# A conditional matrix product and a LoRA layer: the first condition matrices are loaded straight to their places, the others split a pair at a time by GpSimd

## The chip, the cores and the metric

The kernel runs on one NeuronCore of a Trainium2 chip. The core's engines are named as the profile names them: PE (TensorE, matrix products; PEld are its weight loads), DVE (VectorE), ACT (ScalarE), POOL (GpSimd) and SP (SyncE, which here only issues DMAs). The names with a q behind (ACTq, POOLq) are an engine's sequencer: DMA issues, register loads. The metric is the device time of one execution in microseconds (us).

## What is computed

```
W = weights[condition]                       # 16 matrices 64x64; one of them per batch item, 64 items
y = einsum('bct,bcd->bdt', x, W)             # x is (64, 64, 1024)
logits = y @ gate_w.T                        # 8 experts; the best two, softmax over the two
result = y @ base_w.T + base_b               # 1024 x 1024
result += 2 * sum_e w_full[e] * (y @ lora_A[e].T) @ lora_B[e].T
out = x + result
```

## The kernel before, in words

Two batch items of 64 channels make a pair of 128 rows; there are 32 pairs, n = 4j + c. For each pair PE makes three kinds of product. The **mix** multiplies x by the condition matrices into the PSUM tensor `mixed`. The **projection** (`project`, L594) multiplies y by the 1160 columns of `proj_w` (1024 of the base layer, 128 of LoRA, 8 gates), in 8 blocks k of 128 rows and 3 banks b. The **experts** (L626) add the LoRA part. To keep the precision of float32 with faster fp32r products, each operand is split into a high and a low part (`w_hi`, `w_lo`, `y_hi`, `y_lo`), and three products are made: 72 matrix products of 384 or 392 columns for each pair.

Pairs 0 and 1 are mixed in another way than the rest (`mix_first`, L600): plain float32, x as the weights, a block-diagonal matrix `w_pair` of the two condition matrices as the moving side. Pairs from 2 on (`mix`, L614) have x split into `x_parts` by ACT (`x_high`, L323) and DVE (`x_low`, L424), and `w_sel`, the high and low part of one condition matrix side by side. y then comes out turned, with the low part's share in other partitions: ACT copies that to `y_rest` (`rest`, L328), DVE adds it (`add_rest`, L432), ACT moves 16 pieces (`move`, L336), DVE turns them (`turn`, L440), ACT rounds (`y_high`, L355), DVE subtracts (`y_low`, L447).

All engines run code written out by hand, ordered by semaphores; an engine's instructions run in the order of the code. `step(j, c)` of each engine handles projection n, while the mix of pair n + 1 and the output of pair n - 1 go on beside it. In step n PE first makes the first half of mix n + 1 (for n = 1 only after block k = 0), then waits until DVE's `finish` (L508 for banks 0 and 1, L511 for bank 2) has taken pair n - 2 out of the accumulators, of which there are two sets, and projects.

At the start, SP issues the loads in this order: the conditions `cond_sb`, x of pair 0, block 0 of `w_raw`, x of pair 1, blocks 1 to 7, x of pairs 2 and 3, `lb_raw`, `bias`. ACT issues the load of all condition matrices, `cw` (128 x 1024, 512 KB: the 16 matrices side by side, twice one above the other). PE runs 12 products of zeros (L719) meanwhile. When `cw` has landed, GpSimd and DVE copy the matrices of pairs 0 and 1 into `w_pair` (L278, L520; 64 x 64 each), ACT rounds all of `cw` into `cw_parts` (L359) and DVE subtracts (L524). From then on GpSimd's `select` (L259) copies two 128 x 128 pieces, high and low together, for each pair.

Of the kernel before, what the change touches and what calls it, by code (L numbers as in the profile page):

```python
# [13 lines left out]
P = 128  # L14
# [4 lines left out]
def adaln_ffn_kernel(  # L19
# [47 lines left out]
    with ExitStack() as ctx:  # L67
# [14 lines left out]
        cw = sb("cw", [P, cond_w.shape[1]], F32)  # L82
        cw_parts = sb("cw_parts", [P, 2, cond_w.shape[1]], F32R)
        cond_sb = sb("cond_sb", [1, B], I32)
# [6 lines left out]
        x_parts = sb("x_parts", [P, 2, 2, T], F32R)  # L91
        w_pair = sb("w_pair", [P, 2, P], F32)
        w_sel = sb("w_sel", [P, 2, 2, P], F32R)

# [43 lines left out]
        w_first = sem("w_first")  # L138
        first_lower = sem("first_lower")
        first_upper = sem("first_upper")  # L140
        cw_hi_ready = sem("cw_hi_ready")
        cw_ready = sem("cw_ready")
        ident_zero = sem("ident_zero")
# [5 lines left out]
        x_split = sem("x_split")  # L149
        sel_ready = sem("sel_ready")  # L150
        rest_ready = sem("rest_ready")
        sum_done = sem("sum_done")

        moved = sem("moved")
# [22 lines left out]
        lora_done = sem("lora_done")  # L177
        bias_added = sem("bias_added")
        res_ready = sem("res_ready")

# [13 lines left out]
        WARM = 12  # L194
        CW_HALVES = (slice(0, CONDITIONS * CH // 2), slice(CONDITIONS * CH // 2, CONDITIONS * CH))

        @block.sync
        def _(sp):
            sp.dma_start(cond_sb[:, :], condition).then_inc(cond_in, 16)

            def load_x(j, c):
# [3 lines left out]
            for k in range(KT):  # L205
                sp.dma_start(w_raw[:, k, :], w_blocks[k]).then_inc(w_in[k], 16)
                if k == 0:
                    load_x(0, 1)
            load_x(0, 2)
            load_x(0, 3)  # L210
            sp.dma_start(lb_raw[:, :], lora_b).then_inc(lb_in, 16)
# [30 lines left out]
        def _(pool):  # L242
# [10 lines left out]
            def select(j, c):  # L253

                pool.wait_ge(mix_done, 8 * j + 2 * (c - 2) + 2)
                for b in range(2):
                    cond = pool.value_load(cond_sb[0:1, bass.ds(8 * j + 2 * c + b, 1)], min_val=0,
                                           max_val=CONDITIONS - 1)
                    nc.gpsimd.tensor_copy(w_sel[:, c % 2, b, :].rearrange("p (h d) -> p h d", d=CH),  # L259
                                          cw_parts[:, :, bass.ds(cond * CH, CH)]).then_inc(sel_ready, 1)  # L260

            def add_bias(j, c):
                if c >= 4:
# [6 lines left out]


            pool.wait_ge(cond_in, 16)
            lower = [pool.value_load(cond_sb[0:1, 2 * c:2 * c + 1], min_val=0, max_val=CONDITIONS - 1)
                     for c in range(2)]
            pool.wait_ge(cw_in, 16)
            pool.wait_ge(w_zero, 1)
            for c in range(2):
                nc.gpsimd.tensor_copy(w_pair[0:CH, c, 0:CH], cw[0:CH, bass.ds(lower[c] * CH, CH)]) \  # L278
                    .then_inc(first_lower, 1)
            pool.wait_ge(first_lower, 2)  # L280
            pool.wait_ge(cw_ready, 2)
            select(0, 2)
# [19 lines left out]
        def _(act):  # L302
            act.dma_start(cw[:, :], cond_w).then_inc(cw_in, 16)

# [51 lines left out]

            act.wait_ge(cw_in, 16)
            for cols in CW_HALVES:
                nc.scalar.copy(cw_parts[:, 0, cols], cw[:, cols]).then_inc(cw_hi_ready, 1)  # L359
            y_high_first(0, 0)  # L360
            w_high(0)
            y_high_first(0, 1)
# [8 lines left out]
            x_high(0, 2, first=True)  # L371
            x_high(0, 3, first=True)

            act.wait_ge(w_ready, 2)

            def step(j, c, ahead=True, split=True):
                if ahead:
                    rest(j, c + 1, 0)
                if c == 1:
                    act.wait_ge(lb_in, 16)  # L380
                    nc.scalar.copy(lb_hi[:, :], lb_raw[:, :]).then_inc(lb_hi_ready, 1)
                gate_exp(j, c - 1)
                if ahead:
                    if c >= 2:
                        act.wait_ge(turned, 8 * j + 2 * (c - 2) + 2)
                    move(j, c + 1, 0, range(3))
                    rest(j, c + 1, 1)
                    move(j, c + 1, 0, range(3, 8))
                lowT_high(j, c - 1)
                if ahead:  # L390
                    move(j, c + 1, 1, range(8)).then_inc(moved, 1)
                    y_high(j, c + 1, 0)
                    y_high(j, c + 1, 1)
                if split:
                    x_high(j, c + 3)
# [12 lines left out]
        def _(dve):  # L408
# [89 lines left out]
            def finish(j, c):  # L498
                n = 4 * j + c + 1
                dve.wait_ge(lora_done, n)  # L500
                dve.wait_ge(bias_added, n)
                add_bank(c, slice(0, 2))
                add_bank(c, 2).then_inc(res_ready, 1)

            def add_bank(c, b):
                if type(b) is slice:
# [4 lines left out]
                return nc.vector.tensor_tensor(part, acc[:, c % 2, b, 0:hi - lo], part, ALU.add)  # L511


            dve.wait_ge(cond_in, 16)
            upper = [dve.value_load(cond_sb[0:1, 2 * c + 1:2 * c + 2], min_val=0, max_val=CONDITIONS - 1)
                     for c in range(2)]
            dve.wait_ge(cw_in, 16)
            dve.wait_ge(w_zero, 1)
            for c in range(2):
                nc.vector.tensor_copy(w_pair[CH:P, c, CH:P], cw[CH:P, bass.ds(upper[c] * CH, CH)]) \  # L520
                    .then_inc(first_upper, 1)
            for i, cols in enumerate(CW_HALVES):
                dve.wait_ge(cw_hi_ready, i + 1)
                nc.vector.tensor_tensor(cw_parts[:, 1, cols], cw[:, cols], cw_parts[:, 0, cols].bitcast(F32),  # L524
                                        ALU.subtract).then_inc(cw_ready, 1)

# [61 lines left out]
        def _(pe):  # L588
# [15 lines left out]
            def mix(j, c, b):  # L604
                n2 = 8 * j + 2 * (c - 2)
                pe.wait_ge(x_split, n2 + b + 1)
                pe.wait_ge(sel_ready, n2 + b + 1)
                if b == 1 or c >= 3:
# [21 lines left out]
            def first_step():  # L630
# [7 lines left out]
                for k in range(KT):  # L638
# [11 lines left out]
                    if k == 0:  # L650
                        pe.wait_ge(x_in[1], 16)
                        pe.wait_ge(first_lower, 2)
                        pe.wait_ge(first_upper, 2)
                        mix_first(1, 0)

                        pe.wait_ge(y_ready, 2)
                        mix_first(1, 1)
                        with_w_lo(0)
# [4 lines left out]
            def step(j, c, ahead=True):  # L663
# [3 lines left out]
                if c >= 2:  # L667

                    pe.wait_ge(res_ready, s - 1)
                for k in range(KT):  # L670
                    if k % HALF_K == 0:
                        pe.wait_ge(y_ready, 2 * s + k // HALF_K + 1)
                    for product in range(3):
                        for b in range(3):
                            done = project(c, k, b, product)

# [43 lines left out]
            pe.wait_ge(x_in[0], 16)  # L720
            pe.wait_ge(first_lower, 1)
            pe.wait_ge(first_upper, 1)
            mix_first(0, 0)
# [41 lines left out]
```

## Time and profile before

| | us |
|---|---|
| median of 3 runs | 498.06 |
| lowest, highest | 498.01, 498.44 |
| the profiled execution: time | 497.86 |
| its span (first to last instruction) | 495.7 |
| PE busy in the span | 491.1 (99%) |
| ACT, DVE, POOL busy | 380.5, 362.6, 123.7 |

PE's clock was granted in full over the whole span. Times below are from the start of the span. Of the profiled execution's 497.86 us, 2.2 lie outside the span. PE is busy nearly all the time, so the few stretches in which it waits, and the time at which its first product starts, are what the other engines can change.

### The profile page before, as it was taken

To read this page: it belongs to the slowest core of one execution; us is meant where nothing else is said; L and a number is where in the kernel's file an instruction comes from. 1 tells how busy PE (TensorE), PEld (TensorE's weight loads), DVE (VectorE), ACT (ScalarE), POOL (GpSimd) and SP (SyncE) were. 2 spreads that over 40 slices of the span, in tenths; PEclk is the share of its full clock that TensorE was granted. 3 is DMA by queue.
4 is the path that set the end of the run, shared out by engine and by line. 5 is a ranking of instruction groups with operands and counts; after the bars stand their busy time and mean duration, and the time that the engine had idled before them with its cause. 6 is when DMAs were issued, how large, how long until landed. Compare 5 with 4: busy or idle time off the path is not lost.

```text
span 495.7 us, 8620 instructions
## 1 busy us (share of the span) xinstructions
PE 491.1 (99%) x2800; PEld 482.8 (97%) x2800; DVE 362.6 (73%) x771; ACT 380.5 (77%) x740; POOL 123.7 (25%) x111
## 2 busy tenths in 40 slices
PE   8999999999999999999999999999999999999997
PEld 8999999999999999999999999999999999999997
DVE  4977878778777778787777777787877777877653
ACT  4888777878778887778787788787788877887620
POOL 2033311333203333113332123331133330233130
PEclk9999999999999999999999999999999999999999
DMA  8812112122122121121221221211211211211112
GB/s 334 347 42 88 56 72 86 43 87 86 42 85 84 43 85 59 68 85 46 81 85 42 85 85 42 85 70 57 85 59 68 85 49 78 85 42 44 45 42 85
DMA packets 11105, 40.07 MB, mean 81 GB/s; under 512 B 1234, under 2 KB 1618, under 8 KB 11090
## 3 DMA queue, kind: packets, MB, share of 16 engines
q1 hardware_dynamic: 10946, 39.36, 21.3%
q10 hardware_dynamic: 144, 0.52, 0.3%
q8 instruction: 8, 0.13, 0.1%
q14 instruction: 7, 0.06, 0.0%
HBM read 23.10 MB, written 16.78 MB: 80 GB/s over the span
## 4 chain that ended last, share of the span: by engine, by line
PE 97%; ACT 2%; DVE 1%; issue 0%; POOL 0%; ACTq 0%; POOLq 0%
PE acc L594 80%; PE acc L626 9%; PE mixed L614 6%; ACT y_moved L336 1%; PE acc L719 1%; PE acc L620 1%; PE mixed L600 1%; ACT w_raw L328 0%; DVE w_raw L508 0%; DVE w_raw L511 0%; DVE y_turned L440 0%; ACT y_hi L355 0%; ACT y_hi L313 0%; ACT w_hi L309 0%; ACT lowT_hi L348 0%
## 5 line engine op out<-in xcount | busy, mean ns | idle before, releaser
L336 ACT COPY y_moved<-w_raw 32x256 f32<-32x256 f32 x480 | 194.2, 405 | 38.4 <-DVE w_raw L432 32.3
L594 PE MATMUL acc<-w_hi,y_hi 128*128 128x384 f32 (+1 forms) x768 | 182.2, 342 | 0.6 <-ACT w_hi L309 0.3
L594 PE MATMUL acc<-w_hi,y_lo 128*128 128x384 f32 (+1 forms) x768 | 179.1, 338 | 0.0
L594 PE MATMUL acc<-w_lo,y_hi 128*128 128x384 f32 (+1 forms) x768 | 179.0, 338 | 0.0
L268 POOL TENSOR_TENSOR w_raw<-x_sb,bias 128x1024 f32<-128x1024 f32 x32 | 77.3, 2417 | 353.8 <-DVE low L488 267.1
L594 PEld LDWEIGHTS acc<-w_hi,y_hi 128*128 128x128 f32 x768 | 135.4, 188 | 8.3 <-issue 0.8
L594 PEld LDWEIGHTS acc<-w_hi,y_lo 128*128 128x128 f32 x768 | 138.5, 188 | 0.1
L594 PEld LDWEIGHTS acc<-w_lo,y_hi 128*128 128x128 f32 x768 | 138.5, 188 | 0.0
L432 DVE TENSOR_TENSOR w_raw<-mixed,w_raw 64x1024 f32<-64x1024 f32 x60 | 73.0, 1217 | 40.7 <-ACT w_raw L328 40.3
L440 DVE STREAM_TRANSPOSE y_turned<-y_moved 128x512 f32<-128x512 f32 x60 | 39.2, 691 | 53.9 <-ACT y_moved L336 53.9
L424 DVE TENSOR_TENSOR x_parts<-x_sb,x_parts 64x1024 fp32r<-64x1024 f32 x60 | 74.0, 1233 | 1.9
L328 ACT COPY w_raw<-mixed 64x1024 f32<-64x1024 f32 x60 | 60.8, 1013 | 17.7 <-PE mixed L614 16.4
L323 ACT CAST x_parts<-x_sb 64x1024 fp32r<-64x1024 f32 x60 | 62.8, 1047 | 1.2 <-DMA x_sb<-in_x 0.3
L355 ACT CAST y_hi<-y_turned 128x512 fp32r<-128x512 f32 x60 | 36.4, 622 | 25.0 <-DVE y_turned L440 25.0
L259 POOL CAST w_sel<-cw_parts 128x128 fp32r x60 | 46.0, 794 | 3.9 <-PE mixed L600 3.6
L447 DVE TENSOR_TENSOR y_lo<-y_turned,y_hi 128x512 fp32r<-128x512 f32 x60 | 41.2, 686 | 4.5 <-ACT y_hi L355 0.5
L614 PE MATMUL mixed<-x_parts,w_sel 128*128 128x512 f32 x120 | 37.6, 395 | 0.0
L508 DVE TENSOR_TENSOR w_raw<-acc,w_raw 128x768 f32<-128x768 f32 x31 | 29.5, 950 | 1.9 <-PE acc L626 1.9
L626 PE MATMUL acc<-lb_hi,lowT_lo 128*128 128x384 f32 (+1 forms) x96 | 30.6, 319 | 0.0
L626 PE MATMUL acc<-lb_lo,lowT_hi 128*128 128x384 f32 (+1 forms) x96 | 30.5, 318 | 0.0
L626 PE MATMUL acc<-lb_hi,lowT_hi 128*128 128x384 f32 (+1 forms) x96 | 30.4, 317 | 0.0
L614 PEld LDWEIGHTS mixed<-x_parts,w_sel 128*128 128x128 f32 x120 | 21.9, 187 | 0.1
(49 smaller groups left out, 241.5 us busy)
## 6 DMA issues: line engine op xcount, KB each, us to landing
x_sb<-in_x SPq DMA_DIRECT2D x32, 512.0 KB, 3.3
out<-w_raw SPq DMA_DIRECT2D x31, 512.0 KB, 2.6
w_raw<-in_proj_w SPq DMA_DIRECT2D x8, 580.0 KB, 9.6
cw<-in_cond_w ACTq DMA_DIRECT2D x1, 512.0 KB, 3.6
lb_raw<-in_lora_b SPq DMA_DIRECT2D x1, 512.0 KB, 16.3
bias<-in_base_b SPq DMA_DIRECT2D x1, 512.0 KB, 17.0
out<-w_raw SPq DMA_DIRECT2D x2, 192.0 KB, 1.9
out<-w_raw SPq DMA_DIRECT2D x1, 128.0 KB, 2.0
```

The source lines that it names most:

```text
L259: nc.gpsimd.tensor_copy(w_sel[:, c % 2, b, :].rearrange("p (h d) -> p h d", d=CH), cw_parts[:, :, bass.ds(cond * CH, CH)]).then_inc(sel_re ...
L268: nc.gpsimd.tensor_tensor(res[:, c % 4, :], x_sb[:, c % 4, :], bias[:, :], ALU.add) \
L323: nc.scalar.copy(x_parts[half, c % 2, b, :], x_sb[half, c % 4, :]).then_inc(x_hi_ready, 1)
L328: nc.scalar.copy(y_rest[:, b, :], mixed[CH:P, :, :]).then_inc(rest_ready, 1)
L336: done = nc.scalar.copy(y_moved[q * SQ:(q + 1) * SQ, g, :, :], piece.rearrange("m (k q a) -> m q k a", q=QUARTERS, a=SQ)[:, q, :, :])
L424: nc.vector.tensor_tensor(x_parts[there, c % 2, b, :], x_sb[here, c % 4, :], x_parts[here, c % 2, b, :].bitcast(F32), ALU.subtract).then_i ...
L432: nc.vector.tensor_tensor(y_sum[:, b, :].rearrange("m (h t) -> m h t", h=2), mixed[0:CH, :, :], y_rest[:, b, :].rearrange("m (h t) -> m h ...
L440: nc.vector.transpose(y_turned[:, :, ks, :], y_moved[:, :, ks, :]).then_inc(turned, 1)
L447: nc.vector.tensor_tensor(low_part, turned_half(h), high, ALU.subtract).then_inc(y_ready, 1)
L594: return nc.tensor.matmul(acc[:, c % 2, b, 0:hi - lo], y_part[:, c % 2, k, :], w_part[:, k, lo:hi], start=(k == 0 and product == 0), stop= ...
L614: last = nc.tensor.matmul(mixed[:, h, :], w_sel[:, c % 2, b, :], x_parts[:, c % 2, b, h * 512:(h + 1) * 512], start=True, stop=True)
L626: last = nc.tensor.matmul(acc[:, c % 2, b, 0:hi - lo], low_part[:, :], lb_part[:, lo:hi], start=False, stop=(low_part is lowT_lo), skip_gr ...
```

## The change

1. The conditions are loaded by a DMA that ACT issues, not SP. ACT then makes one small copy (`exps` from `zeros`), reads the four conditions of pairs 0 and 1 into registers one after another, and after each read issues a DMA of that one 64 x 64 matrix from DRAM into its corner of `w_pair` (16 KB, 256 bytes in a row). PE's `mix_first` waits for `first_in` in place of the copies of GpSimd and DVE.
2. `cw` is loaded by SP behind x of pair 2. `cw_parts` and the four instructions that filled it are gone, and so are the four copies into `w_pair`.
3. `select` now takes from `cw`: for each of the two matrices one copy with rounding into the high half of `w_sel` and one plain copy into `cw_two` (128 x 64 each), and then one subtraction for both (128 x 128 in all), behind a wait on `two_ready`. These are five instructions in place of two. PE's `mix` waits for the whole pair.
4. ACT: block 0 of `w_hi` comes ahead of `y_high_first(0, 0)`; `lb_hi` is made ahead of step 1, not in it behind `rest(2, 0)`.
5. DVE signals `banks_added` behind banks 0 and 1; PE starts a step's projection on that, and waits for `res_ready` only ahead of the first product into bank 2.

```diff
@@ sync
-            sp.dma_start(cond_sb[:, :], condition).then_inc(cond_in, 16)
             load_x(0, 2)
+            sp.dma_start(cw[:, :], cond_w).then_inc(cw_in, 16)
             load_x(0, 3)
@@ gpsimd, select
                     cond = pool.value_load(cond_sb[0:1, bass.ds(8 * j + 2 * c + b, 1)], min_val=0,
                                            max_val=CONDITIONS - 1)
-                    nc.gpsimd.tensor_copy(w_sel[:, c % 2, b, :].rearrange("p (h d) -> p h d", d=CH),
-                                          cw_parts[:, :, bass.ds(cond * CH, CH)]).then_inc(sel_ready, 1)
+                    nc.gpsimd.tensor_copy(w_sel[:, c % 2, b, 0:CH], cw[:, bass.ds(cond * CH, CH)]) \
+                        .then_inc(two_ready, 1)
+                    nc.gpsimd.tensor_copy(cw_two[:, b, :], cw[:, bass.ds(cond * CH, CH)]).then_inc(two_ready, 1)
+                pool.wait_ge(two_ready, 16 * j + 4 * (c - 2) + 4)
+                high = w_sel[:, c % 2, :, 0:CH]
+                nc.gpsimd.tensor_tensor(w_sel[:, c % 2, :, CH:P], cw_two[:, :, :], high.bitcast(F32), ALU.subtract) \
+                    .then_inc(sel_ready, 1)
@@ gpsimd, start
             pool.wait_ge(cond_in, 16)
-            lower = [pool.value_load(cond_sb[0:1, 2 * c:2 * c + 1], min_val=0, max_val=CONDITIONS - 1)
-                     for c in range(2)]
             pool.wait_ge(cw_in, 16)
-            pool.wait_ge(w_zero, 1)
-            for c in range(2):
-                nc.gpsimd.tensor_copy(w_pair[0:CH, c, 0:CH], cw[0:CH, bass.ds(lower[c] * CH, CH)]) \
-                    .then_inc(first_lower, 1)
-            pool.wait_ge(first_lower, 2)
-            pool.wait_ge(cw_ready, 2)
             select(0, 2)
@@ scalar
-            act.dma_start(cw[:, :], cond_w).then_inc(cw_in, 16)
+            act.dma_start(cond_sb[:, :], condition).then_inc(cond_in, 16)
+
+            act.wait_ge(zeros_ready, 1)
+            nc.scalar.copy(exps[:, :], zeros[:, 0:NE])
+
+            act.wait_ge(w_zero, 1)
+            act.wait_ge(cond_in, 16)
+            for c in range(2):
+                for b in range(2):
+                    cond = act.value_load(cond_sb[0:1, 2 * c + b:2 * c + b + 1], min_val=0, max_val=CONDITIONS - 1)
+                    half = slice(b * CH, (b + 1) * CH)
+                    act.dma_start(w_pair[half, c, half], cond_w[half, bass.ds(cond * CH, CH)]) \
+                        .then_inc(first_in[c], 16)
...
-            act.wait_ge(cw_in, 16)
-            for cols in CW_HALVES:
-                nc.scalar.copy(cw_parts[:, 0, cols], cw[:, cols]).then_inc(cw_hi_ready, 1)
+            w_high(0)
             y_high_first(0, 0)
-            w_high(0)
             y_high_first(0, 1)
...
             x_high(0, 3, first=True)
+            act.wait_ge(lb_in, 16)
+            nc.scalar.copy(lb_hi[:, :], lb_raw[:, :]).then_inc(lb_hi_ready, 1)
@@ vector
-                add_bank(c, slice(0, 2))
+                add_bank(c, slice(0, 2)).then_inc(banks_added, 1)
                 add_bank(c, 2).then_inc(res_ready, 1)
...
-            for c in range(2):
-                nc.vector.tensor_copy(w_pair[CH:P, c, CH:P], cw[CH:P, bass.ds(upper[c] * CH, CH)]) \
-                    .then_inc(first_upper, 1)
-            for i, cols in enumerate(CW_HALVES):
-                dve.wait_ge(cw_hi_ready, i + 1)
-                nc.vector.tensor_tensor(cw_parts[:, 1, cols], cw[:, cols], cw_parts[:, 0, cols].bitcast(F32),
-                                        ALU.subtract).then_inc(cw_ready, 1)
@@ tensor
             def mix(j, c, b):
-                pe.wait_ge(sel_ready, n2 + b + 1)
+                pe.wait_ge(sel_ready, 4 * j + c - 1)
...
-                    pe.wait_ge(res_ready, s - 1)
+                    pe.wait_ge(banks_added, s - 1)
...
+                            if k == 0 and product == 0 and b == 2 and c >= 2:
+                                pe.wait_ge(res_ready, s - 1)
...
-            pe.wait_ge(first_lower, 1)
-            pe.wait_ge(first_upper, 1)
+            pe.wait_ge(first_in[0], 32)
```

How the instructions stand now on ACT, from the start of the program to block 1 of `w_hi`, before:

```order
L303 DMA cw<-in_cond_w 128x1024
L359 ACT_TABLE_LOAD
L359 CAST cw_parts<-cw 128x512 [waits cw_in]
L359 CAST cw_parts<-cw 128x512
L313 CAST y_hi<-mixed 128x512 [waits mix_done]
L309 CAST w_hi<-w_raw 128x384 [waits w_in0]
L313 CAST y_hi<-mixed 128x512 [waits mix_done]
```

and of after (TENSOR_LOAD and ISA are the read of a condition into a register and the sums for the address; two of the four rounds are shown):

```order
L297 DMA cond_sb<-in_condition 1x64
L300 ACT_TABLE_LOAD
L300 COPY exps<-zeros 128x8 [waits zeros_ready]
L306 TENSOR_LOAD cond_sb [waits cond_in,w_zero]
L306 ISA x2
L308 ISA
L308 DMA w_pair<-in_cond_w 64x64
L306 TENSOR_LOAD cond_sb
L306 ISA x2
L308 ISA
L308 DMA w_pair<-in_cond_w 64x64
```

Four rounds of register read and DMA issue now stand ahead of ACT's first work on y and w, and the DMA of `cw` has left this queue.

On POOL, behind the constants of the start, before (`cond_sb` is read twice for pairs 0 and 1, then twice for pair 2):

```order
L278 COPY w_pair<-cw 64x64
L278 ISA
L278 COPY w_pair<-cw 64x64
L257 TENSOR_LOAD cond_sb [waits mix_done,cw_ready,first_lower]
L257 ISA x2
L259 ISA
L259 COPY w_sel<-cw_parts 128x128
L257 TENSOR_LOAD cond_sb
L257 ISA x2
L259 ISA
L259 COPY w_sel<-cw_parts 128x128
L268 TENSOR_TENSOR w_raw<-x_sb,bias 128x1024 [waits mix_done,x_in0,low_ready,bias_in]
```

and of after:

```order
L255 TENSOR_LOAD cond_sb [waits mix_done,cw_in,cond_in]
L255 ISA x2
L257 ISA
L257 COPY w_sel<-cw 128x64
L259 COPY cw_two<-cw 128x64
L255 TENSOR_LOAD cond_sb
L255 ISA x2
L257 ISA
L257 COPY w_sel<-cw 128x64
L259 COPY cw_two<-cw 128x64
L262 TENSOR_TENSOR w_sel<-cw_two,w_sel 128x2x64 [waits two_ready]
L271 TENSOR_TENSOR w_raw<-x_sb,bias 128x1024 [waits mix_done,x_in0,low_ready,bias_in]
```

The selection for pair 2 grew from two to five instructions, and waits for `cw_in`, whose DMA is now the twelfth that SP issues.

## Rows read from the trace of the kernel before

**Rows 1.** The page, chain of work that ended last: shares by engine.

```profile
PE 97%; ACT 2%; DVE 1%; issue 0%; POOL 0%; ACTq 0%; POOLq 0%
```

**Rows 2.** The chain in order of time (start us, duration us, what), 0 to 60.

```profile
28.71 1.01 ACT w_raw L328
...
37.53 0.95 DVE w_raw L508
38.48 0.34 DVE w_raw L511
```

**Rows 3.** Timeline of the start (start, duration in us; in brackets idle before, releaser).

```profile
0.80 0.39 ACTq L303 DMA_DIRECT2D cw<-in_cond_w  x1
1.22 1.28 ACT L359 ACT_TABLE_LOAD   x1 [1.22 <-PEq L757]
5.67 2.05 PE L600 MATMUL mixed<-w_pair,x_sb 128*128 128x128 f32 x16
8.01 0.77 PE L594 MATMUL acc<-w_hi,y_hi 128*128 128x384 f32 x3 [0.28 <-ACT w_hi L309]
```

**Rows 4.** Register reads on DVE's and POOL's queue, by source line (ns; first, last start).

```profile
L515 DVEq TENSOR_LOAD <-cond_sb x2: 315/433/551, 2.1 to 3.0; - x2
...
L257 POOLq TENSOR_LOAD <-cond_sb x60: 283/290/299, 7.8 to 451.1; - x60
```

**Rows 5.** DMA issues and us to landing, windows 0.7 to 1.0 and 6.2 to 6.5.

```profile
cw<-in_cond_w ACTq DMA_DIRECT2D x1, 512.0 KB, 3.6
...
x_sb<-in_x SPq DMA_DIRECT2D x1, 512.0 KB, 13.5
```

**Rows 6.** Timeline of ACT around step 1.

```profile
22.33 2.12 ACT L323 CAST x_parts<-x_sb 64x1024 fp32r<-64x1024 f32 x2 [0.31 <-DMA x_sb<-in_x]
25.14 1.01 ACT L328 COPY w_raw<-mixed 64x1024 f32<-64x1024 f32 x1 [0.69 <-PE mixed L614]
26.18 1.05 ACT L381 CAST lb_hi<-lb_raw 128x1024 fp32r<-128x1024 f32 x1
```

**Rows 7.** Timeline of DVE: the split of the weights, of x, the first gates.

```profile
8.99 1.35 DVE L411 TENSOR_TENSOR w_lo<-w_raw,w_hi 128x1160 fp32r<-128x1160 f32 x1
11.20 4.24 DVE L411 TENSOR_TENSOR w_lo<-w_raw,w_hi 128x1160 fp32r<-128x1160 f32 x3 [0.85 <-ACT w_hi L309]
17.83 3.91 DVE L411 TENSOR_TENSOR w_lo<-w_raw,w_hi 128x1160 fp32r<-128x1160 f32 x3
21.77 2.47 DVE L424 TENSOR_TENSOR x_parts<-x_sb,x_parts 64x1024 fp32r<-64x1024 f32 x2
24.43 0.22 DVE L458 TENSOR_TENSOR ties<-logits_sb 128x64 f32<-128x64 f32 x1
45.62 1.23 DVE L424 TENSOR_TENSOR x_parts<-x_sb,x_parts 64x1024 fp32r<-64x1024 f32 x1
```

**Rows 8.** Timeline of POOL, then the tile w_sel in window 45.7 to 47.1.

```profile
8.54 0.29 POOL L259 CAST w_sel<-cw_parts 128x128 fp32r x1 [3.55 <-PE mixed L600]
9.21 1.29 POOL L259 CAST w_sel<-cw_parts 128x128 fp32r x1 [0.38 <-issue]
28.74 2.40 POOL L268 TENSOR_TENSOR w_raw<-x_sb,bias 128x1024 f32<-128x1024 f32 x1 [18.24 <-PE mixed L614]
...
L259 POOL CAST w_sel<-cw_parts x2: 282/784/1287, 45.5 to 45.7; 128x128 fp32r x2
```

**Rows 9.** Timeline of PE (PEld: its weight loads) at the mixes.

```profile
24.24 0.37 PEld L614 LDWEIGHTS mixed<-x_parts,w_sel 128*128 128x128 f32 x2
37.96 0.63 PE L614 MATMUL mixed<-x_parts,w_sel 128*128 128x512 f32 x2
38.87 0.79 PE L594 MATMUL acc<-w_hi,y_hi 128*128 128x384 f32 x3 [0.27 <-DVE w_raw L511]
53.69 0.63 PE L614 MATMUL mixed<-x_parts,w_sel 128*128 128x512 f32 x2
54.16 0.69 PE L594 MATMUL acc<-w_hi,y_hi 128*128 128x384 f32 x3
```

More of the change, by code:

```diff
@@ L82, in adaln_ffn_kernel @@
         cw = sb("cw", [P, cond_w.shape[1]], F32)
-        cw_parts = sb("cw_parts", [P, 2, cond_w.shape[1]], F32R)
         cond_sb = sb("cond_sb", [1, B], I32)
@@ L92, in adaln_ffn_kernel @@
         w_pair = sb("w_pair", [P, 2, P], F32)
+        cw_two = sb("cw_two", [P, 2, CH], F32)
         w_sel = sb("w_sel", [P, 2, 2, P], F32R)
@@ L138, in adaln_ffn_kernel @@
         w_first = sem("w_first")
[L139 to L142, printed above, removed]
+        first_in = [sem(f"first_in{c}") for c in range(2)]
         ident_zero = sem("ident_zero")
@@ L149, in adaln_ffn_kernel @@
         x_split = sem("x_split")
-        sel_ready = sem("sel_ready")
         rest_ready = sem("rest_ready")
         sum_done = sem("sum_done")
+        two_ready = sem("two_ready")
+        sel_ready = sem("sel_ready")
         moved = sem("moved")
@@ L178, in adaln_ffn_kernel @@
         bias_added = sem("bias_added")
+        banks_added = sem("banks_added")
         res_ready = sem("res_ready")
@@ L194, in adaln_ffn_kernel @@
         WARM = 12
-        CW_HALVES = (slice(0, CONDITIONS * CH // 2), slice(CONDITIONS * CH // 2, CONDITIONS * CH))
         @block.sync
         def _(sp):
-            sp.dma_start(cond_sb[:, :], condition).then_inc(cond_in, 16)
             def load_x(j, c):
@@ L378, in step @@
                     rest(j, c + 1, 0)
-                if c == 1:
-                    act.wait_ge(lb_in, 16)
-                    nc.scalar.copy(lb_hi[:, :], lb_raw[:, :]).then_inc(lb_hi_ready, 1)
                 gate_exp(j, c - 1)
@@ L511, in add_bank @@
                 return nc.vector.tensor_tensor(part, acc[:, c % 2, b, 0:hi - lo], part, ALU.add)
[L514 to L518, printed above, removed]
-            for c in range(2):
-                nc.vector.tensor_copy(w_pair[CH:P, c, CH:P], cw[CH:P, bass.ds(upper[c] * CH, CH)]) \
-                    .then_inc(first_upper, 1)
-            for i, cols in enumerate(CW_HALVES):
-                dve.wait_ge(cw_hi_ready, i + 1)
-                nc.vector.tensor_tensor(cw_parts[:, 1, cols], cw[:, cols], cw_parts[:, 0, cols].bitcast(F32),
-                                        ALU.subtract).then_inc(cw_ready, 1)
             dve.wait_ge(w_in[0], 16)
@@ L651, in first_step @@
                         pe.wait_ge(x_in[1], 16)
-                        pe.wait_ge(first_lower, 2)
-                        pe.wait_ge(first_upper, 2)
+                        pe.wait_ge(first_in[1], 32)
                         mix_first(1, 0)
```

## The prediction

> **What bounds the kernel now.** I read first the shares of the chain that ended last: 97% of it is PE [rows 1]. In steady work PE waits for nobody: at the step border at 53.69 us the mix starts and the projection follows 0.47 us later, with no idle time noted, while DVE has been done for a while [rows 9]. So what other engines do in the loop costs nothing as long as it stays beside PE. The question is only when PE gets through its first steps. There I followed the chain in order of time and looked for where it leaves PE [rows 2]: before 8.01 us (start-up), and from 28.71 to 38.82 us, where it runs through ACT and DVE: the second `rest` of pair 2, its moves, the turn, and `finish` of pair 0 up to 38.82. PE's projection of pair 2 starts there at 38.87, and without that wait it would have started 0.47 us behind the mix, at 37.96 + 0.47 = 38.43 [rows 9]. I call this start S2. Whatever delays S2 delays the end by the same amount, since all that follows is PE at work. The change touches only things ahead of it.
>
> **Part 1, the first mix.** Before, PE starts it at 5.67, at once behind the products of zeros [rows 3], so the loads and copies of the condition matrices were hidden there; an earlier arrival can win nothing. After, ACT's queue decides. Its table load ends at 1.22 + 1.28 = 2.50 [rows 3]. The condition values were readable at 2.1 [rows 4]; ACT reads the first at about 2.6. Between the two reads on DVE's queue lie 0.9 us [rows 4], on POOL a read at 7.8 leads to a copy at 8.54 [rows 4, 8]: 0.75 for a read with its address, say 0.8 for the first and 0.65 for the next. A DMA issue took 0.39 [rows 3]. So the second issue starts at 2.6 + 0.8 + 0.4 + 0.65 = 4.45, the fourth at about 6.55. How long 16 KB take to land among the big loads no row shows. From below, the condition load: issued at 0.80, readable at 2.1, 1.3 us with the engines empty [rows 3, 4]; from above, the 512 KB of `cw` at 3.6 us [rows 5]. The size is that of the first, the traffic that of the second; I take 2.0. That puts the first mix at 6.5 (bounds 5.8 to 8.0), d = 0.8 later than before.
>
> The page "DMA: Bandwidth & Descriptors" of the Trainium skill (section "Anatomy of one DMA") puts a fixed cost of about 2.0 us on one DMA, for the GpSimd path; by it the mix would start at 6.45. The condition load above, on the hardware path, took 1.3, so the trace does not bear the figure out for an idle chip.
>
> PE's product at 8.01 waited 0.28 for ACT's block 0 of `w_hi` [rows 3]. `cw` no longer stands ahead of x and w, so that block is there 512 KB, some 1.3 us, earlier, and ACT makes it first: the 0.28 goes, down to the 0.14 or so that a change of product costs. Later PE gaps of about 0.3 us go as well, since blocks 1 to 3 also land earlier. PE then reaches the first mix of pair 2 at 24.24 + 0.8 - 0.14 - 0.3 = 24.6, where it was at 24.24 [rows 9]. DVE's split of the weights had to wait 0.85 us for `w_hi` of block 1 [rows 7]; that wait takes up the later start, so its last split and the split of x for pair 2 stay where they are: w_lo to 21.74, x from 21.77 to 24.24 [rows 7]. The removed splits of `cw` on ACT and DVE lay in idle time ahead of 6.4 us and give nothing.
>
> **Part 2, the selection for pair 2.** Before, POOL did it at 8.5 to 10.5 [rows 8] and PE used it at 24.24: 14 us of cover. After, it needs `cw`, which takes in SP's queue the place behind x of pair 2. Byte for byte that is the place which x of pair 2 had before (`cw` then went ahead), and this landed 13.5 us after its issue at 6.34, at 19.84 [rows 5]. Add the read of the condition, 0.75: the first copy is ready to run at 20.6. Four copies of 128 x 64 at 0.25 each (a bit under the 0.28 of a 128 x 128 cast [rows 8]), and a subtraction at 0.4 (an eighth of the 2.40 us of the 128 x 1024 addition [rows 8] plus its start): if nothing interferes, the pair is ready at about 22.3, and PE waits for nothing.
>
> But something does. The cast at 9.21 took 1.29 us and ended 0.16 after DVE's w_lo (8.99 to 10.34) [rows 7, 8]. In the loop the first cast takes 282 ns, the second 1287, over the 1.23 us of DVE's split of x at 45.62 [rows 7, 8]. All 30 pairs show this, as the mean over the 60 casts is 0.79. So a POOL instruction that starts while DVE works on two SBUF tensors ends only when DVE's does. From 17.83 to 24.24 DVE does such work without a break [rows 7]. At best POOL gets one instruction in at each DVE border: copy 1 behind w_lo at 21.74, copy 2 behind 22.98, copy 3 behind 24.24. If DVE keeps its place, all five come behind 24.24. Copies 3 and 4 then end at 24.4 and 24.65, the subtraction at 25.1 if it finds a gap between the comparisons of the first gates, which start at 24.43 and take 0.22 each [rows 7]. With 0.2 for those and 0.1 to 0.2 for what DVE itself is held up: 25.45. Without turns at the borders: some 25.8. PE loads its weights at **25.5** instead of 24.24. That is the term on which the sum rests, 1.25 us.
>
> The page "SBUF — State Buffer" of the Trainium skill (section "SBUF: two separate sides") calls the port pair of the two an exclusive lock held for a whole instruction, either way round; by it DVE, too, would stand still for POOL's copies, and the x split of pair 2 would end at 24.24 + 2 x 0.16 = 24.55, PE's start at 25.8. The trace shows little of that side: the split at 45.62 began beside a running cast and took 1.23.
>
> **Part 3, the rest.** `lb_hi` on ACT now stands ahead of `rest(2, 0)`. x of pair 3 lands where it did, its casts end at 24.45, `lb_hi` takes 1.05 [rows 6], so ACT is free at 25.5. Before, `rest` started at 25.14 [rows 6]; with the mix at 25.5 it can't start before 26.4, so this is hidden. If the mix were not late, it would cost 0.4. `banks_added`: S2 then waits for DVE's 38.48 instead of 38.82 [rows 2], with 0.05 for the signal 38.53 instead of 38.87; PE's own limit is 38.43. That is a gain of 0.33 at S2 and none later, where PE does not wait. The extra wait on bank 2 comes 0.36 us (two products) behind and is met about then. In the loop the five POOL instructions come to 2 to 3.5 us where two took 1.5; the selection made in one step is used at the next step's start, 8 us later, so it costs nothing. DVE's hold-ups in the loop are tenths beside a margin of some 0.7 us.
>
> **The sum.** Chain and PE up to S2 both shift by 1.25, less 0.33: **+0.9 us**. From the profiled execution: 497.86 + 0.9 = 498.8. It is 0.2 below the median of the runs, 498.06, so as a median 499.0. What this measurement can tell from no change is about 0.2%, 1.0 us: the forecast lies just inside.
>
> **Rivals.** (a) *POOL is not held up*, since copies of 64 columns slip in: the selection ends at 22.3, PE starts the mix at 24.6, +0.4; ACT's `lb_hi` makes the same +0.4 on the chain. Less 0.33: +0.1, 498.2. For it: no row shows POOL beside a string of DVE instructions. Against: 30 of 30 pairs of casts. (b) *The small loads are late.* Landing 3.6 us after issue puts the first mix at 8.1, d = 2.4. PE would reach the pair 2 mix at 26.2, DVE's splits end 1.5 later, and POOL finishes behind them at 26.3 to 26.9: +1.7 to +2.3, 500.0. The point from which it decides is d = 1.7. The same case holds PE's clock falling to 1.2 GHz while it idles at 5.7 to 6.5; the granted clock was full before, with no idle time there. This is clearly slower. (c) *Faster.* The best that PE could do is a first mix at 5.67, no gaps (0.44) and no wait at S2 (0.44): 0.9 us, 497.2. But the chain through `lb_hi` stays at +0.4 - 0.33, so a gain needs x of pair 3 to land earlier too, and the bytes ahead of it are the same. (d) *The copies meet DVE luckily*: should `cw` land 0.2 us earlier, or the splits run 0.3 later, one more border falls into POOL's wait and the mix starts at 25.2 or before: +0.6.
>
> **How the numbers follow.** Forecast with (d), +0.4 to +1.4: 0.62, a bit over half of it below +1.0. (a): 0.18. (b): 0.15. (c) by over 1 us: 0.02; unforeseen: 0.03. Within 0.2%: 0.34 + 0.18 = 0.52; slower: 0.28 + 0.15 + 0.03 = 0.46; faster: 0.02. The range runs from (a) with a little gain, 497.9, to (b)'s middle, 500.0.
>
> **What the new profile would show.** Right: `mixed<-w_pair` starts near 6.5; POOL's first `w_sel` copies near 20.6, some of over 1 us; the subtraction ending near 25.4, PE's weight load for the pair 2 mix just behind it with an idle time of about 0.8 put down to POOL; the projection of pair 2 near 39.8; PE idle nowhere later. Wrong: POOL copies of 0.25 us each from 20.6 on; a first mix behind 7.5; a granted clock under 1; or PE waiting in the loop for `w_sel` or `banks_added`.

## The result, and the profile after

The changed kernel took 503.48 us (median of 5 runs, 502.59 to 503.96) against 498.06: ratio 1.0107, 95% interval 1.0095 to 1.0118. It is slower by 5.4 us; the forecast was 499.0, at most 500.0. The profiled execution took 503.90 us, its span is 502.1 us, 6.4 more than before. The runs of the changed kernel spread more than those of before; the mean granted clock was 0.993 in some and 0.997 in others.

The start on the timeline of the changed kernel (start, duration; in brackets the idle time before and what ended it), beside [rows 3]:

```profile
2.20 3.90 SPq L203 DMA_DIRECT2D w_raw<-in_proj_w  x7
3.02 4.21 ACTq L308 DMA_DIRECT2D w_pair<-in_cond_w  x4
10.42 3.75 PE L588 MATMUL mixed<-w_pair,x_sb 128*128 128x128 f32 x16 [4.41 <-DMA w_pair<-in_cond_w]
13.82 1.31 PE L582 MATMUL acc<-w_hi,y_hi 128*128 128x384 f32 x3
```

The first mix starts at 10.42, not 5.67, after 4.41 us in which PE waited for the small loads, and takes 3.75 in place of 2.05. The chain in order of time shows which load (second of four):

```profile
4.34 5.95 DMA w_pair<-in_cond_w
10.29 0.14 issue
10.42 3.75 PE mixed L588 x16
```

Issued at 4.34 (forecast 4.45), it landed 5.95 us later. The stretches (busy us of PE, PEld, DVE, ACT, POOL, then PE's granted clock, DMA share, GB/s) show the clock:

```profile
7.00:9.00 2.00, 0.00 (x0) 0.00 (x0) 0.00 (x0) 0.51 (x1) 0.00 (x0) 0.93 1.02 396
9.00:12.00 3.00, 1.58 (x7) 1.61 (x8) 0.00 (x0) 0.00 (x0) 0.00 (x0) 0.50 1.02 402
12.00:16.00 4.00, 4.00 (x20) 4.00 (x19) 1.86 (x3) 2.38 (x4) 0.00 (x0) 0.56 1.02 418
16.00:20.00 4.00, 4.00 (x31) 4.00 (x30) 4.00 (x4) 4.00 (x6) 0.00 (x0) 1.00 1.03 414
```

After its idle time PE was granted 0.50, the 1.2 GHz level, from before its first mix until some point in 12 to 16 us. Where the difference arises is read from the starts of the same work in both traces:

| start of | before | after | difference |
|---|---|---|---|
| first mix | 5.67 | 10.42 | 4.75 |
| projection of pair 0 | 8.01 | 13.82 | 5.81 |
| mix of pair 2 | 24.42 | 30.73 | 6.31 |
| projection of pair 2 | 38.87 | 44.86 | 5.99 |
| projection of pair 3 | 54.16 | 60.48 | 6.32 |
| span | 495.7 | 502.1 | 6.4 |

All of it is there by the mix of pair 2. The 0.32 that `banks_added` wins at pair 2's projection is lost again by the next one. The selection for pair 2 began at 20.99 (forecast 20.6) and was held up as forecast, or worse, but PE came so late that it did not matter:

```profile
20.99 0.24 POOL L257 CAST w_sel<-cw 128x64 fp32r x1 [18.80 <-issue]
21.16 1.43 POOL L259 COPY cw_two<-cw 128x64 f32 x1
22.54 0.23 POOL L257 CAST w_sel<-cw 128x64 fp32r x1
22.72 0.23 POOL L259 COPY cw_two<-cw 128x64 f32 x1
23.04 4.21 POOL L262 TENSOR_TENSOR w_sel<-cw_two,w_sel 128x128 fp32r<-128x128 f32 x1
30.73 0.63 PE L602 MATMUL mixed<-x_parts,w_sel 128*128 128x512 f32 x2
```

The subtraction alone lasted 4.21 us, to 27.25; PE wanted the result at 30.7.

### The profile page after: what moved, and what is told of

The parts are those of the page before. It is cut to its first block, busy times and chain, and to the rows that moved or that the text cites. A ratio compares the mean times of both kernels' runs of the same rounds, so it can differ in the third digit from the quotient of the medians.

```text
span 502.1 us, 8754 instructions
## 1 busy us (share of the span) xinstructions
PE 493.5 (98%) x2800; PEld 485.5 (97%) x2800; DVE 362.4 (72%) x767; ACT 379.1 (76%) x739; POOL 178.2 (35%) x199
## 4 chain that ended last, share of the span: by engine, by line
PE 95%; ACT 2%; DMA 1%; DVE 1%; ACTq 0%; issue 0%
PE acc L582 79%; PE acc L614 9%; PE mixed L602 6%; DMA w_pair<-in_cond_w 1%; PE mixed L588 1%; ACT y_moved L342 1%; PE acc L608 1%; DVE w_raw L434 0%; ACTq L306 0%; ACT w_raw L334 0%; DVE w_raw L510 0%; DVE w_raw L513 0%; ACTq L308 0%; DVE y_turned L442 0%; ACT L300 0%
## 5 line engine op out<-in xcount | busy, mean ns | idle before, releaser
L426 DVE TENSOR_TENSOR x_parts<-x_sb,x_parts 64x1024 fp32r<-64x1024 f32 x60 | 75.7, 1262 | 1.9
L262 POOL TENSOR_TENSOR w_sel<-cw_two,w_sel 128x128 fp32r<-128x128 f32 x30 | 41.2, 1374 | 2.4
L257 POOL CAST w_sel<-cw 128x64 fp32r x60 | 34.9, 582 | 18.8 <-issue 18.8
```

Source lines behind the costliest of these rows:

```text
L262: nc.gpsimd.tensor_tensor(w_sel[:, c % 2, :, CH:P], cw_two[:, :, :], high.bitcast(F32), ALU.subtract) \
L426: nc.vector.tensor_tensor(x_parts[there, c % 2, b, :], x_sb[here, c % 4, :], x_parts[here, c % 2, b, :].bitcast(F32), ALU.subtract).then_i ...
```

## The experiments

Two things had to be found: why 16 KB took 5.9 us to land, and what each of the other terms is worth by itself.

**SP holds its loads back.**

```diff
                 if k == 0:
+                    sp.wait_ge(first_in[0], 32)
+                    sp.wait_ge(first_in[1], 32)
                     load_x(0, 1)
```

> The changed kernel, but SP holds all loads behind x of pair 0 and block 0 of the weights until the four small loads have landed. Theory (the small loads stand behind what SP has already issued; in the changed kernel their first packet came at 7.0, 4.0 us after the first issue, and pair 0's two landed at 10.3): with 1.1 MB ahead of them in place of 2.8 MB they land at 5.5 to 7, so mixed<-w_pair starts there. Rival (rows of 256 bytes, or an address from a register, are slow of themselves): they land 5 to 6 us after issue as before, the first mix stays at 10 or later. Either way the loads held back come late, and PE will wait for block 1 of the weights (near 13): by the theory some 501 us, by the rival over 506.

Measured: 502.89 us, ratio 1.0093 (1.0076 to 1.0110). The loads of `w_pair` and the first mix:

```profile
DMA to landing us min/median/max: 1.9/2.0/2.7
...
6.39 2.02 PE L590 MATMUL mixed<-w_pair,x_sb 128*128 128x128 f32 x16
...
12.04 3.18 PE L590 MATMUL mixed<-w_pair,x_sb 128*128 128x128 f32 x16 [2.24 <-DMA x_sb<-in_x]
```

The same instructions, rows of 256 bytes and registers, landed in 2.0 us, and the first mix started at 6.39. So neither the small rows nor the register addresses are what took 5.9 us, but the company of the other loads. The total gains little, as the loads held back now come late: the mix of pair 1 waits 2.24 us for x, and in the profiled execution the clock falls there instead (0.68 between 12 and 14 us). The 501 us I expected underrated that.

**More held-back loads: SP holds from block 2 on** (the same two waits stand ahead of block 2, behind x of pairs 0 and 1 and blocks 0 and 1).

> As the run in which SP held its loads back, but SP holds from block 2 of the weights on: 2.2 MB ahead of the small loads and nothing behind them. If the bytes ahead alone count, the first packets come near 7 as in the changed kernel (2.2 MB take 5.4 us at 410 GB/s, from 2.1), and pair 0's land at 8 to 8.5, since nothing shares the engines with them; if what SP issues afterwards is what delays them, they land at 6 to 6.5 as with 1.1 MB ahead. Total 503 or above, as the weights come late.

Measured: 503.29 us, ratio 1.0109 (1.0089 to 1.0129), first mix at 9.77. ACT's queue (q10) in the windows 6.5 to 7, 7 to 7.5 and 7.5 to 8 us, as packets, MB and share of the 16 engines:

```profile
q10 hardware_dynamic: 6, 0.00, 1.4%
...
q10 hardware_dynamic: 19, 0.00, 4.2%
...
q10 hardware_dynamic: 201, 0.04, 40.2%
```

No packet of ACT's queue ran between 3 and 6.5 us, though its first load was issued at 3.03. The first came when all but some 0.3 of the 2.2 MB that SP had issued were through (2.0 MB by 7 us). With 1.1 MB ahead (the run before) the first ones came between 4.5 and 5 us; in the changed kernel between 7 and 7.5. So what SP has already issued holds the start back, and 2.2 MB do so for longer than 1.1 MB. Beyond that the start no longer follows the bytes: in the changed kernel SP had issued block 2 as well (at 2.67), 2.8 MB in all, and ACT's first packets ran when 2.0 MB were through, not 2.8. What sets this limit the runs do not show. The page "DMA: Bandwidth & Descriptors" of the Trainium skill (section "Queues, rings and completion order") says that each DMA engine takes turns between queues, packet by packet. By that the small loads would have begun soon after their issue; the measurement decides, and here they did not, though their packets did mix with SP's once both ran. Pair 0's loads landed later than I expected (9.6 rather than 8 to 8.5): nearly all packets had run by 8.5, and the landing hung on the last 18 of ACT's queue, between 8.5 and 9.5.

In the changed kernel a second thing may be added. While SP's later loads run beside them, few of the small packets get through (window 7 to 8 us):

```profile
q1 hardware_dynamic: 93, 0.37, 93.7%
q10 hardware_dynamic: 65, 0.01, 6.8%
```

65 in 1 us, beside 93 of SP's, against 201 in half a microsecond with SP's queue nearly empty. A load of 64 rows is some 80 packets. Of the 5.95 us, 2.7 had passed when the first packets ran, past 7; in the other 3.3 the two loads of pair 0 were worked off. How much of the 3.3 is the slow mixing these runs do not part: see the run with GpSimd below.

**The loads issued earlier, with fixed addresses.** This kernel always takes the matrices of conditions 0 to 3 and leaves out the reading of the conditions.

```diff
-            act.wait_ge(zeros_ready, 1)
-            nc.scalar.copy(exps[:, :], zeros[:, 0:NE])
-
             act.wait_ge(w_zero, 1)
-            act.wait_ge(cond_in, 16)
...
-                    cond = act.value_load(cond_sb[0:1, 2 * c + b:2 * c + b + 1], min_val=0, max_val=CONDITIONS - 1)
...
-                    act.dma_start(w_pair[half, c, half], cond_w[half, bass.ds(cond * CH, CH)]) \
+                    act.dma_start(w_pair[half, c, half], cond_w[half, (2 * c + b) * CH:(2 * c + b + 1) * CH]) \
```

> The changed kernel with fixed addresses for the four small loads (it takes the matrices of conditions 0 to 3, so the output of pairs 0 and 1 is not the reference's), issued by ACT at 1.4 to 3.5 with no register read ahead. Nothing else differs. Theory (place behind SP's issued loads): the first pair's loads, issued 1.6 us sooner with about 1.6 MB ahead, land some 3 us sooner, near 7; the first mix at 7, no or a short fall of the clock; total about 499.5 to 500.5, and now GpSimd's selection for pair 2, held up by DVE's string of splits, should become what the pair 2 mix waits for. Rival (rows of 256 bytes are slow): 5.9 us from issue, landing 7.9 for pair 0's second; the two are near each other, the packets' first start decides: by the theory it is over 3 us behind the issue, by the rival under 2.

Measured: 500.22 us (499.26 to 500.78), ratio 1.0044 (1.0028 to 1.0061).

```profile
1.36 2.49 ACTq L303 DMA_DIRECT2D w_pair<-in_cond_w  x4
...
7.79 2.02 PE L583 MATMUL mixed<-w_pair,x_sb 128*128 128x128 f32 x16 [1.25 <-DMA w_pair<-in_cond_w]
...
25.43 0.51 POOL L262 TENSOR_TENSOR w_sel<-cw_two,w_sel 128x128 fp32r<-128x128 f32 x1
...
26.04 0.70 PE L597 MATMUL mixed<-x_parts,w_sel 128*128 128x512 f32 x2
```

2.6 us sooner at the first mix, no fall of the clock after 1.25 us of idle time in this execution (in two of the four runs the mean granted clock was 0.997), and 3.3 us less in the end. Landing still took up to 6.2 us from issue. The first packets part the theories. They ran between 4.5 and 5 us, over 3 us behind the issue at 1.36, as the first theory asked. The same half microsecond held the first packets of the run in which SP held its loads back, where ACT had issued at 3.03. ACT's queue in the window 4 to 5 us here, and in 4.5 to 5 us there:

```profile
q10 hardware_dynamic: 24, 0.01, 2.5%
...
q10 hardware_dynamic: 30, 0.01, 6.3%
```

Both have 1.1 MB ahead. With 1.7 us between the issues and the same start, it is the bytes ahead that count here, not the time since issue. As expected before the run, the subtraction of the selection ends at 25.94 and PE's mix starts right behind it.

**GpSimd issues the small loads** (the reads and DMAs moved from ACT's code to GpSimd's).

> The changed kernel with the four reads and small loads made by GpSimd in place of ACT. Theory A (the wait for the first packet lies in what ACT's and SP's DMA issues share): GpSimd's descriptors are made elsewhere, the first packet comes 1 to 2 us behind the issue, landing near 6 to 7, total 499 to 500.5. Theory B (it lies in the DMA engines, which work off the bytes ahead): first packet 4 us behind the issue as before, landing 9 to 10.5, total 502.5 to 504.

Measured: 503.33 us, ratio 1.0109 (1.0092 to 1.0125). First mix and, for window 7 to 8 us, the software queue:

```profile
10.50 3.75 PE L587 MATMUL mixed<-w_pair,x_sb 128*128 128x128 f32 x16 [5.02 <-DMA w_pair<-in_cond_w]
...
q0 software_dynamic: 21, 0.01, 4.0%
```

The first issue was at 3.77, the first packet past 7.5, and the first mix at the same time as from ACT. Which engine issues the loads makes no difference to that: theory B. Together with the held-back runs this puts the wait behind what SP had already handed over, not in what ACT and SP share when they issue. Two rows limit the theory. SP had issued 3.4 MB before 3.77, and the first packet ran when 2.1 MB were through, so again not all bytes ahead count. And a load is only 32 packets on this queue, not 80, yet each of the four landed 5.0 to 5.4 us after its issue; between 8.4 and 8.8 us none of their packets ran, though the second load had been issued at 4.97. So the slow working off of small packets is at most a small part of the landing time here, and its share in the changed kernel is not shown.

**SP issues them, in its own queue.**

```diff
                 if k == 0:
                     load_x(0, 1)
+                    sp.wait_ge(w_zero, 1)
+                    sp.wait_ge(cond_in, 16)
+                    for c in range(2):
+                        for b in range(2):
+                            cond = sp.value_load(cond_sb[0:1, 2 * c + b:2 * c + b + 1], min_val=0,
+                                                 max_val=CONDITIONS - 1)
+                            half = slice(b * CH, (b + 1) * CH)
+                            sp.dma_start(w_pair[half, c, half], cond_w[half, bass.ds(cond * CH, CH)]) \
+                                .then_inc(first_in[c], 16)
```

> The changed kernel with the four reads and small loads made by SP, between the loads of x of pair 1 and of block 1 of the weights, in place of ACT; the same bytes, rows and registers. Theory (a load is served behind the bytes that were issued before it, 1.6 MB here, on whatever queue): issued at 2.2 to 6.2, pair 0's two land near 7, the first mix at 7, the clock stays full; block 1 lands near 10.3, about as before; total 499 to 499.8. Rival (small rows among big loads are slow on any queue): landing over 5 us after issue, first mix over 8.5, total over 501.

Measured: 501.12 us, ratio 1.0064 (1.0048 to 1.0081).

```profile
3.22 4.34 SPq L213 DMA_DIRECT2D w_pair<-in_cond_w  x4
7.60 3.76 SPq L203 DMA_DIRECT2D w_raw<-in_proj_w  x7
7.90 3.63 PE L589 MATMUL mixed<-w_pair,x_sb 128*128 128x128 f32 x16 [2.30 <-DMA w_pair<-in_cond_w]
```

With 1.6 MB ahead and nothing behind, the landing took 1.8 to 3.6 us, not over 5 as by the rival. But no big load ran beside most of these packets, so the run says little on small rows among big loads. I was wrong on two sizes: SP issued the first load at 3.22, not at about 2.2, so that the mix came at 7.90, not 7; and after 2.30 us of waiting the clock had fallen, so that it took 3.63 in place of 2.0. These two, 0.9 and 1.6 us, are more than the 1.3 by which the total is above 499.8.

**More products of zeros** (`WARM = 22` in place of 12).

> The changed kernel with 22 products of zeros in place of 12, so that PE works until about 9.2 and idles for 1 us, not 4.4, ahead of the first mix. Theory: the granted clock stays full, the first mix takes 2.05 in place of 3.75 us and the next products their usual time; 1.8 us less than the changed kernel: 501.6. Rival (the clock's fall is an effect that other waits hide): no change, 503.4.

Measured: 502.64 us (501.93 to 503.07), ratio 1.0090 (1.0073 to 1.0106).

```profile
10.52 2.02 PE L588 MATMUL mixed<-w_pair,x_sb 128*128 128x128 f32 x16 [1.72 <-DMA w_pair<-in_cond_w]
...
28.77 0.70 PE L602 MATMUL mixed<-x_parts,w_sel 128*128 128x512 f32 x2
```

The first mix comes no sooner, but takes 2.02, and the mix of pair 2 starts at 28.77, 1.96 us before the 30.73 of the changed kernel. So the half clock costs 2.0 us where it lasts as in the profiled execution. The medians differ by only 0.84, with spreads of over 1 us on both sides; the profiled executions (502.30 and 503.90) by 1.6. I had expected 501.6: in two of this kernel's four runs the mean granted clock was 0.997, so more products of zeros did not keep the clock full in each. GpSimd's selection for pair 2 ends at 28.67 here, just ahead of PE's mix, so it has become a limit again.

**`banks_added` alone**, on the kernel before:

```diff
-                    pe.wait_ge(res_ready, s - 1)
+                    pe.wait_ge(banks_added, s - 1)
...
+                            if k == 0 and product == 0 and b == 2 and c >= 2:
+                                pe.wait_ge(res_ready, s - 1)
```

> The kernel before with banks_added alone: PE starts a step's projection when banks 0 and 1 are taken and waits for bank 2 just ahead of its first product. The prediction's term: 0.33 us sooner at the start of pair 2's projection and for good, 497.7. Theory from the trace of the changed kernel (0.33 was gained there, and 0.32 lost at the second half of the next mix, which waits for DVE's add_rest, behind the same finish in DVE's order): the projection of pair 2 starts at 38.5, that of pair 3 at 54.16 as before; no change, 498.1.

Measured: 498.15 us, ratio 1.0002 (0.9993 to 1.0011). The projections of pair 2 and 3, with the mix between them:

```profile
38.42 0.80 PE L595 MATMUL acc<-w_hi,y_hi 128*128 128x384 f32 x3
...
42.01 0.70 PE L615 MATMUL mixed<-x_parts,w_sel 128*128 128x512 f32 x2
...
54.03 0.69 PE L595 MATMUL acc<-w_hi,y_hi 128*128 128x384 f32 x3
```

and the same of the next experiment's kernel, which has no `banks_added`:

```profile
38.74 0.80 PE L592 MATMUL acc<-w_hi,y_hi 128*128 128x384 f32 x3 [0.30 <-DVE w_raw L513]
...
42.01 0.69 PE L612 MATMUL mixed<-x_parts,w_sel 128*128 128x512 f32 x2
...
54.02 0.69 PE L592 MATMUL acc<-w_hi,y_hi 128*128 128x384 f32 x3
```

0.32 us ahead at pair 2's projection, level at the mix that follows, and no difference in the total. PE has only moved its wait from one place to the next that DVE's order sets.

**The selection in five instructions, `cw` still first** (`select` of the changed kernel, the first mix and the load of `cw` as before; the splits of `cw` on ACT and DVE are gone).

> The kernel before, with the selection in five instructions straight from cw; cw is loaded first as before, the first mix is made as before, cw_parts is gone. Theory (in the loop the selection has some 8 us of cover, and the splits of cw at the start lay in idle time): 498.1, no change; POOL busy about 178 us in place of 124. Rival (the longer hold-ups of DVE and POOL cost something in every step): over 499.

Measured: 497.84 us, ratio 0.9996 (0.9987 to 1.0005): no difference that can be told.

**The same, but the selection for pair 2 waits for x of pair 2.**

```diff
             pool.wait_ge(first_lower, 2)
+            pool.wait_ge(x_in[2], 16)
             select(0, 2)
```

> As the last one, but GpSimd waits for x of pair 2 (it landed at 19.84) before it selects for pair 2; the first mix stays at 5.67. This measures the prediction's main term by itself. Theory (GpSimd is held up by DVE's splits): first copy wanted at 20.6, one instruction at the border behind the last w_lo, one behind each split of x, the subtraction over near 25.2; the pair 2 mix 0.9 to 1.0 us later than before, no banks_added to set against it: 499.0. Rival (it isn't held up): done by 22.3, 498.1.

Measured: 498.39 us, ratio 1.0007 (0.9998 to 1.0016) to before, and not the 499.0 that I expected; the median is 0.55 above the last kernel's. In the traces it is clearer:

```profile
20.69 1.19 POOL L260 CAST w_sel<-cw 128x64 fp32r x1 [15.46 <-DMA x_sb<-in_x]
21.83 1.30 POOL L262 COPY cw_two<-cw 128x64 f32 x1
23.09 1.30 POOL L260 CAST w_sel<-cw 128x64 fp32r x1
24.34 0.23 POOL L262 COPY cw_two<-cw 128x64 f32 x1
24.66 0.49 POOL L265 TENSOR_TENSOR w_sel<-cw_two,w_sel 128x128 fp32r<-128x128 f32 x1
25.25 0.70 PE L613 MATMUL mixed<-x_parts,w_sel 128*128 128x512 f32 x2 [0.62 <-issue]
...
55.05 0.69 PE L593 MATMUL acc<-w_hi,y_hi 128*128 128x384 f32 x3
```

Copy by copy this is the forecast's table: ready at 20.6, one instruction behind each long one of DVE, the subtraction over at 25.15. The projection of pair 3 starts at 55.05 against 54.02: 1.03 us, in the span 496.6 against 495.6. The last kernel's profiled execution was one of its shortest (497.37 us), this one's is the median, so the medians' 0.55 is the better measure of what the time loses.

**Half of `cw` first**, meant to beat both: as the kernel with the selection in five instructions, and

```diff
-            act.dma_start(cw[:, :], cond_w).then_inc(cw_in, 16)
+            act.dma_start(cw[0:CH, :], cond_w[0:CH, :]).then_inc(cw_in, 16)
...
+                if k == 3:
+                    sp.dma_start(cw[CH:P, :], cond_w[CH:P, :]).then_inc(cw_up_in, 16)
...
-        WARM = 12
+        WARM = 10
```

> A version meant to beat both. As select, but only the lower 64 rows of cw are loaded first (256 KB; DVE copies the odd items' matrices across to the upper rows of w_pair), the upper 64 rows come behind block 3 of the weights, and there are 10 products of zeros. x of pair 0 and block 0 land 0.6 us sooner. Theory: the first mix at 5.1, the projections at 7.4, everything behind them 0.5 to 0.6 sooner: 497.5. Rival (the wait moves to DVE's and ACT's chain in step 1, whose last inputs, x of pair 3 and lb, land as before): 498.0.

Measured: 499.71 us, ratio 1.0033 (1.0023 to 1.0042), slower than before by 1.7. Landing of the first loads (KB, us) and the first mix:

```profile
x_sb<-in_x SPq DMA_DIRECT2D x1, 512.0 KB, 5.5
cw<-in_cond_w ACTq DMA_DIRECT2D x1, 256.0 KB, 4.9
...
6.73 2.05 PE L602 MATMUL mixed<-w_pair,x_sb 128*128 128x128 f32 x16 [1.04 <-DMA x_sb<-in_x]
```

Half the bytes landed 1.3 us later than all of them had [rows 5], and x of pair 0, issued 1.22, at 6.7 in place of 5.6. A load into 64 partitions is slow not only at the start. When the other half of `cw` ran, at 13 to 14 us, the DMA engines moved 210 GB/s with a busy share of 1.06, against 418 and 413 GB/s at shares of 1.03 and 1.02 at 11 to 12 and at 15 to 16 us. PE then waits 0.38 and 0.63 us for `w_hi` of two later blocks (at 15.74 and 18.22), whose loads ran beside and behind that half. So the first mix is 1.06 us later than before and the mix of pair 2 2.3 us (26.75 against 24.42). Both come from loads into 64 partitions; why these run at half the rate the runs do not show. The rival, a limit in step 1, was not what decided.

## Why the prediction was wrong, point by point

- **The step that failed is the landing of the small loads in part 1.** The forecast took 2.0 us between bounds of 1.3 and 3.6; it took 5.95. With it failed the term that the sum put at nothing, the fall of PE's clock while it waits. The issue times held (4.34 against 4.45 for the second load), and 2.0 us is what they take when SP holds its loads back, with the first mix at 6.39 against the forecast 6.5. The bound from above was no bound: 3.6 us was the landing of `cw` [rows 5], the very first load, with nothing ahead. x of pair 2 took 13.5 [rows 5], and that was the row that showed what a load issued behind many others does. The trace of before even shows that another queue is no way around it. These are ACT's queue (q10) and SP's (q1) in the windows 3.0 to 3.5 and 3.5 to 4.0 us; x of pair 0 had been issued at 1.21 on SP's:

```profile
q10 hardware_dynamic: 50, 0.20, 101.6%
...
q10 hardware_dynamic: 40, 0.10, 52.2%
q1 hardware_dynamic: 23, 0.09, 45.7%
```

  In the first of them nothing of SP's queue ran: x waited until `cw`, issued 0.4 us sooner, was nearly through.
- **Rival (b) was the right mechanism, and too small by size and chance (0.15).** It put the first mix at 8.1 and the total at 500.0. It named the fall of the clock only as a companion; that costs 2.0 us in the traces (0.8 between the medians). Both of its signs, a first mix behind 7.5 and a granted clock under 1, are in the new profile.
- **The sum, redone:** 4.75 (late first mix) and 2.0 (clock), less some 0.4 for gaps that went (as part 1 had them): 6.3, against 6.31 at the mix of pair 2 and 6.4 in the span. The median's 5.4 is lower; two of the five runs had a mean clock of 0.997 and not 0.993, so less time at the low clock, and these are the two shortest (502.59 and 503.14).
- **The selection for pair 2, the forecast's main term,** was right as a mechanism, against rival (a): 1.03 us by itself in the traces and 0.55 between the medians, 1.25 forecast. In the changed kernel it costs nothing, because PE is later still. In the run with the loads issued early PE's mix starts 0.1 us behind its end, so there it is a limit again.
- **A turn at every border of DVE's instructions** was only partly right. Behind the splits of x GpSimd got one each time. Between consecutive `w_lo` it got none: the subtraction of the changed kernel began at 23.04, beside DVE's three `w_lo` from 23.02 to 26.93, and ended at 27.25. In the run with more products of zeros a cast of 128 x 64 begun at 22.90 took 2.50 us, past one border of `w_lo` and to the end of the last at 25.31. The page "SBUF — State Buffer" of the Trainium skill (section "SBUF: two separate sides") says that the two engines hold the port pair for a whole instruction. The ends agree, each of these just behind the end of an instruction of DVE's; who is next at a border these runs show only for these cases.
- **`banks_added` at 0.33 for good** was wrong: 0.32 us won at one place, none left at the next. I looked at the wait that it shortens and not at the next one that hangs on the same DVE chain (`add_rest` comes behind `finish` in DVE's order).
- **In the loop, and the splits of `cw` at nothing:** right (0.9996, interval 0.9987 to 1.0005). The move of `lb_hi` was not tried by itself; in the changed kernel ACT was idle 3.0 us behind it.

## What to carry to other kernels

A small load is not quick because it is small: what has been issued ahead of it, on any queue, holds it back, here up to about 2 MB and 4 us. Read its landing from a row of a load issued at that moment, not from the first load of the kernel. And when a matrix that a copy fetched from a large early load is instead fetched by a dependent load of its own (load an index, read it, load the row), that second load is issued behind the very traffic that the change was meant to relieve; 512 KB at the head were cheaper here than 64 KB behind 2 MB. Where PE idles ahead of its first real product, the clock's fall can come on top.

## What the runs showed of the hardware that I had not expected

- The first packets of loads on ACT's queue came when the 1.1 MB issued ahead on SP's were through (between 4.5 and 5 us, whether issued at 1.36 or 3.03), or nearly all of 2.2 MB (6.5 to 7). With 2.8 MB ahead, or 3.4 MB and GpSimd's queue, they came when 2.0 or 2.1 MB were through (past 7 and 7.5).
- Among running loads of rows of 4 KB and more, 65 to 73 packets of ACT's small loads got through in a microsecond; with the other queue nearly empty, 201 in half a microsecond.
- A GpSimd subtraction of 128 x 128 took 0.5 us in one place and 4.21 us beside a string of DVE instructions on two SBUF tensors.
- In the profiled executions PE kept the full clock after 1.25 and 1.72 us without work, and after 2.2, 2.3 and 4.4 us it was granted 1.2 GHz. It was not so in every run: the mean clock was 0.997 in two of four runs of each kernel with the short waits, and 1.000 in two of four of the kernel with 2.2 us.
- 256 KB into 64 partitions landed in 4.9 us, 512 KB into 128 in 3.6, both as first load of the kernel; later such a load moved 210 GB/s with the DMA engines busy all the time, about half of what loads into 128 partitions moved around it.
